# A two-layer gated cross-attention block: six of eight batches' projections moved in among the first half groups of the attention

## The chip, the cores and the metric

The kernel runs on one core of a Trainium2 chip. The metric is the device time of one execution in microseconds. The core has TensorE (PE; its weight loads are shown apart as PEld), VectorE (DVE), ScalarE (ACT), GpSimd (POOL) and SyncE (SP, which here only issues DMAs). Each runs its own instructions strictly in the order in which they are written, and waits where a semaphore has not reached its value.

## The reference

Two gated layers on x (8 batches, 512 tokens, 256 features) with a context of the same shape:

```python
x = x + tanh(g_xattn[0]) * pruned_attention(layernorm(x), ctx)      # 16 heads of 16
x = x + tanh(g_ffn[0])   * fp4_swiglu(layernorm(x))                 # weights and inputs on an FP4 grid
x = x + tanh(g_xattn[1]) * linear_attention(ctx, layernorm(x))      # then a layer norm
x = x + tanh(g_ffn[1])   * int8_linear(layernorm(x))
```

Pruned attention is `softmax(q k^T / 4)`; of its 512 columns the 460 with the largest column sums are kept, the other 52 are zeroed, and the result is multiplied with v. In the linear attention `kv = k^T v` depends on the context alone, so each batch has one 256x256 matrix (`m`) and a row (`r`) that the feed-forward part multiplies with.

## The kernel before

The program has four stages. `prepare` loads and transposes the weights. `project` computes, batch by batch, q, k and v of the attention and the matrix `m` of the linear attention, and writes them to scratch memory in HBM. `attend` and `feed` share one block, `attend_and_feed`: the attention, and behind it the feed-forward units, whose first ones overlap the attention's tail.

**The projection (`project`, L427 to L778).** It is its own block with its own pools: it uses all eight PSUM banks (`psT` two for transposes, `psP` four for products, `psE` two for the matrix part). For one batch TensorE transposes normalized x (L508), computes x1 of the previous batch (L526, L529), transposes the context (L508), multiplies q (L514), kv of the previous batch (L538), k (L514), m of the previous batch (L548 to L553), v (L578) and the gram matrix of the context (L584). ScalarE evacuates xT, cT, the high (fp16) part of q and k, and the gram matrix; VectorE writes the low part (`parts`, L629), v (L690), the statistics and the normalized x (`norm`, L604 to L623), and the small matrix operations. `Fp4Weights` rounds the feed-forward weights to the FP4 grid among this: `scales` on VectorE behind batch 0, `round` (four VectorE operations for a third of the weights) in batches 1, 6 and 7, `split` (two operations) on GpSimd, and at the very end `transposes` on TensorE with `copies` on ScalarE and VectorE.

**The attention (`attend`).** The unit is a half group z, of which there are 256: two 128x512 score tiles in `ps_a`. For each z TensorE makes the first scores (L920), VectorE their negated row maxima (L991), ScalarE two exponentials with row sums (L1090). Every second z, TensorE adds column sums into `ps_c` (L947) with weights from VectorE's reciprocal (L1002). After 16 half groups (one unit) VectorE ranks the column sums in steps of one operation per z (L1034 to L1050) to find the 52 dropped ones. The second scores (L920 into `ps_b`, with shift and drop rows added), their exponential (L1098) and the product with v (L962) of half group z run `LAG = 42` half groups later. So in the first 42 steps, the head, there are first scores only, `ps_b` and `ps_v` are idle, and so is most of TensorE. All engines run the same loop:

```python
            for z in range(at.last):
                step(z)
                n = z - tail
```

SyncE's part (`at.sync`) loads q and k of unit u (`load`, L862), v (`load_values`, L867), and places the shift and drop rows (L877, L885). The first four buffers of q and k are set to 1.0 first: two memsets on VectorE (L984, L985), six on GpSimd.

## Time and profile before

| | |
|---|---|
| median of 3 runs | 1329.58 us (1328.76 to 1330.57) |
| profiled execution, its own time | 1333.29 us |
| its span, first to last instruction | 1331.6 us, mean granted clock 0.927 |
| TensorE busy in the span | 1063.7 us (80%) |
| VectorE busy | 1046.6 us (79%) |
| ScalarE busy | 871.1 us (65%) |
| GpSimd busy | 119.5 us (9%) |

The stages by the trace: `prepare` to 20.4 us, `project` with the FP4 transposes from 20.4 to 229.4, the first score of the attention at 240.9, the first second score at 320.7, the last exponential of first scores at 805.3, the feed-forward part to the end. "Busy" is the time in which an engine has an instruction; a busy TensorE is not TensorE at its peak, and its speed depends on the granted clock, which is 1.0 (2.4 GHz) or 0.5 (1.2 GHz).

### The profile page before, as it was taken

How to read it: one execution, taken by the hardware profiler on the slowest of the kernel's cores; microseconds unless marked ns; L12 is line 12 of the kernel's file. 1: busy time of each engine (PE TensorE's matmuls, PEld its weight loads, DVE VectorE, ACT ScalarE, POOL GpSimd, SP SyncE). 2: the span in 40 equal slices, each digit the busy share in tenths (PEclk: the TensorE clock that was granted, in tenths of full speed). 3: DMA queues.
4: the chain of work that ended last, by engine and by line, in shares of the span. 5: the costliest groups of instructions: out<-in, count | busy, mean ns of one | idle time of the engine just before them, and what ended most of it. 6: DMA issues, size and time to landing. Idle time of an engine off the chain costs nothing.

```text
span 1331.6 us, 17557 instructions
## 1 busy us (share of the span) xinstructions
PE 1063.7 (80%) x5688; PEld 511.6 (38%) x5688; DVE 1046.6 (79%) x2095; ACT 871.1 (65%) x1896; POOL 119.5 (9%) x111
## 2 busy tenths in 40 slices
PE   4999996577677777677777775788999999999985
PEld 3667774011111111111111111234667676676663
DVE  3675664588888988888888885546799999999975
ACT  2232322577999999999999994575454555555542
POOL 0030226200000000000000000000111111110111
PEclk7999997555999999999999998788999999999987
DMA  7444331211121112222221101011011111111000
GB/s 231 137 146 159 136 124 43 48 33 33 30 41 28 32 38 41 42 41 42 41 41 35 36 18 49 15 37 40 25 48 40 33 52 44 32 37 36 25 16 32
DMA packets 77887, 71.77 MB, mean 54 GB/s; under 512 B 13738, under 2 KB 71396, under 8 KB 77796
## 3 DMA queue, kind: packets, MB, share of 16 engines
q1 hardware_dynamic: 77796, 70.65, 19.9%
q8 instruction: 46, 0.75, 0.2%
q14 instruction: 45, 0.37, 0.1%
HBM read 42.83 MB, written 27.28 MB: 53 GB/s over the span
## 4 chain that ended last, share of the span: by engine, by line
ACT 34%; PE 33%; issue 7%; DVE 6%; SPq 1%; DMA 1%; POOL 0%; ACTq 0%; DVEq 0%
ACT ea L1090 20%; ACT prob L1098 13%; PE ps_a L1306 11%; PE ps_b L1265 6%; PE ps_c L1265 4%; PE ps_v L1265 2%; PE ps_a L1286 2%; PE ps_c L947 2%; DVE nmax L991 2%; PE ps_a L1315 1%; PE ps_b L920 1%; PE ps_v L962 1%; PE ps_a L920 1%; PE ps_b L1361 1%; PE ps_c L1258 1%
## 5 line engine op out<-in xcount | busy, mean ns | idle before, releaser
L1090 ACT ACTIVATE ea<-ps_a,nmax 128x512 f32<-128x512 f32 x512 | 362.6, 748 | 31.9 <-DVE nmax L991 31.8
L991 DVE TENSOR_REDUCE nmax<-ps_a 128x2 f32<-128x1024 f32 x256 | 312.9, 1223 | 70.5 <-PE ps_a L920 68.9
L1098 ACT ACTIVATE prob<-ps_b 128x1024 f32<-128x1024 f32 x256 | 279.2, 1091 | 48.7 <-PE ps_b L920 48.7
L920 PE MATMUL ps_b<-q_st,k_st 52*128 52x512 f16 x512 | 102.5, 396 | 143.6 <-ACT prob L1098 143.5
L1306 PE MATMUL ps_a<-wgu,xT 128*128 128x352 f32 x512 | 164.9, 467 | 2.5 <-ACT xT L1430 2.3
L920 PEld LDWEIGHTS ps_b<-q_st,k_st 52*128 52x128 f16 x512 | 25.1, 93 | 368.9 <-ACT prob L1098 336.6
L947 PE MATMUL ps_c<-ea,rz 128*32 128x512 f32 x1024 | 153.7, 676 | 1.1 <-DVE rank L1034 1.1
L962 PE MATMUL ps_v<-prob,v_in 128*16 128x512 f32 x1024 | 137.0, 607 | 11.6 <-DVE att L1058 11.4
L1090 ACT ACTIVATION_READ_ACCUMULATOR ea<-ps_a,nmax 128x1 f32 x512 | 136.2, 266 | 0.0
L920 PE MATMUL ps_a<-k_st,q_st 48*128 48x512 f16 x512 | 108.1, 419 | 31.3 <-ACT ea L1090 18.4
L1306 PEld LDWEIGHTS ps_a<-wgu,xT 128*128 128x128 f32 x512 | 94.7, 192 | 50.4 <-issue 5.1
L1443 ACT ACTIVATE ea<-ps_a 128x352 f32<-128x352 f32 x128 | 59.4, 464 | 76.3 <-PE ps_a L1306 76.2
L1265 PE MATMUL ps_b<-wdn,hT 128*128 128x256 f32 (+1 forms) x384 | 97.1, 392 | 0.0
L1251 POOL TENSOR_TENSOR rs_a<-ve_a,half 128x4 f32<-128x4 f32 x20 | 20.2, 1012 | 755.3 <-DVE ve_a L1576 755.3
L1039 DVE MAX8 top<-rank 128x8 f32<-128x512 f32 x112 | 76.6, 684 | 0.2
L1045 DVE MATCH_REPLACE8 rank<-top,rank 128x512 f32<-128x512 f32 x112 | 75.7, 676 | 0.0
L1265 PEld LDWEIGHTS ps_b<-wdn,hT 128*128 128x128 f32 (+1 forms) x384 | 66.6, 189 | 21.9 <-issue 15.9
L1254 POOL TENSOR_TENSOR rs_b<-ve_b,half 128x4 f32<-128x4 f32 x19 | 37.6, 1978 | 263.6 <-DVE ve_b L1592 263.6
L920 PEld LDWEIGHTS ps_a<-k_st,q_st 48*128 48x128 f16 x512 | 26.0, 96 | 75.5 <-ACT ea L1090 55.6
L1614 DVE SCALAR_TENSOR_TENSOR ea<-ea 128x512 f32<-128x512 f32 (+1 forms) x32 | 36.9, 1155 | 10.7 <-ACT ea L1425 5.8
L962 PEld LDWEIGHTS ps_v<-prob,v_in 128*16 128x16 f32 x1024 | 17.6, 94 | 65.7 <-issue 61.7
L947 PEld LDWEIGHTS ps_c<-ea,rz 128*32 128x32 f32 x1024 | 21.0, 112 | 55.7 <-issue 55.7
(233 smaller groups left out, 1622.8 us busy)
## 6 DMA issues: line engine op xcount, KB each, us to landing
q_scr<-q_p SPq DMA_DIRECT2D x24, 256.0 KB, 2.7
k_scr<-k_p SPq DMA_DIRECT2D x24, 256.0 KB, 2.5
q_st<-q_scr SPq DMA_DIRECT2D x32, 192.0 KB, 4.7
k_st<-k_scr SPq DMA_DIRECT2D x32, 192.0 KB, 5.0
x_in<-in_x SPq DMA_DIRECT2D x8, 512.0 KB, 5.6
c_in<-in_ctx SPq DMA_DIRECT2D x8, 512.0 KB, 4.2
v_scr<-v_s SPq DMA_DIRECT2D x8, 512.0 KB, 2.6
v_in<-v_scr SPq DMA_DIRECT2D x16, 256.0 KB, 3.1
```

Source lines behind the costliest of these rows:

```text
L920: return e.matmul(bank, left[b][o:o + rows, r, t * P:t * P + P], right[b][o:o + rows, r], start=True, stop=True)
L947: e.matmul(ps_c[32 * j:32 * j + 32, :], rz[:, n % TT, n // TT, j], ea[g % RING][:, j], start=(n == 0), stop=(n == GROUPS - 1)).then_inc(s_ ...
L962: e.matmul(ps_v[32 * j:32 * j + DK, :], v_in[u % 2][:, t, o:o + DK], prob[g % RING][:, j], start=(t == 0), stop=(t == TT - 1)).then_inc(s_ ...
L991: e.tensor_reduce(nmax[u % 2][:, t].rearrange("p (h r) -> p r h", h=2)[:, r], ps_a[:, z % 2 * 2:z % 2 * 2 + 2], AX_X, ALU.max, negate=True ...
L1039: e.max(top[:, :], rank[:, :]).then_inc(*dv.up())
L1045: e.match_replace(rank[:, :], top[:, :], rank[:, :], NEG).then_inc(*dv.up())
L1090: e.activation(ea[c % RING][:, g % 4], ps_a[:, g % 4], ACT.Exp, bias=nmax[u % 2][:, t, n:n + 1], accum_out=tot[u % 2][:, t, n:n + 1]).then ...
L1098: e.activation(prob[g % RING][:, 2 * (z % 2):2 * (z % 2) + 2], ps_b[:, :, :], ACT.Exp).then_inc(s_prob, 1)
L1254: e.tensor_tensor(rs_b[p][:, :, :], ve_b[p][:, :, :], half[:, :, :], ALU.pow).then_inc(s_rs_b, 1)
L1265: ins = e.matmul(dst[:, t * D:t * D + D], left(c, t), right(c), start=False, stop=(last and t == N - 1 and c == chunks[-1]))
L1306: ins = e.matmul(gu[:, q % 2, 0:HALF_F], xT[:, c, t * P:t * P + P], w.wgu[:, c, k * HALF_F:(k + 1) * HALF_F], start=(c == 0), stop=(c == D ...
L1443: e.activation(dst[:, t, k % 2 * HALF_F:(k % 2 + 1) * HALF_F], gu[:, q % 2, 0:HALF_F], func).then_inc(s_act_gu, 1)
```

## The change

Everything from the projection on becomes one block. `project` is rewritten as a list of fills. A fill is one piece of work of one PSUM bank: TensorE writes it, ScalarE or VectorE or both take it out, and the next fill of that bank waits for that (`left`). A batch has 16 fills: 0 and 1 xT, 3 and 4 cT, 6 and 7 q, 9 and 10 k, 12 gram, 14 and 15 v, and, for the previous batch, 2 x1, 5 rb, 8 kv, 11 m, 13 row. Fill n uses bank n % 3 of `ps_b[0]`, `ps_b[1]` and `ps_v`, which the attention does not use before step 42. The 32 fills of batches 0 and 1 run first, with all FP4 work beside them, then the FP4 transposes; the other 110 (batches 2 to 7 and the matrix part of batch 7) are spread over steps 0 to 40 of the attention's loop, two or three behind each step.

Other edits: x is normalized in place by ScalarE (`normal`, four 128x256 operations with scale and bias, in two halves) instead of by VectorE, which now also computes the bias `nb`; most double buffers of the projection become single; FP4 rounding works in place; all the feed's and the attention's memory is allocated beside the projection's, except `prob`, which takes its place; the memsets of `q_st` and `k_st` come ahead of the projection on VectorE and GpSimd; GpSimd runs all three splits before the first row of `row_parts`; SyncE's queue interleaves the projection's loads and stores with the attention's first loads; the memset of `ps_v` goes, and the first second scores and the first product with v wait for the last fills of the banks.

```diff
 def build(nc, a, out):
...
-            prepare(nc, ctx, a, w, ey)
-            project(nc, ctx, a, w, ey, scr)
-        attend_and_feed(nc, ctx, a, out, w, scr)
+            prepare(nc, ctx, a, w, ey, [at.ps_a[:, n] for n in range(4)])
+            fp4.with_scales(Mem(nc, early, ctx), [at.ps_a[:, n] for n in range(4)])
+            pj = project(Mem(nc, early, ctx), a, w, ey, scr, [at.ps_b[:, 0], at.ps_b[:, 1], at.ps_v[:, :]])
+        at.prob = [m.sb(f"prob{n}", [P, 4, T]) for n in range(at.ring.shape[1])]
+        fd = feed(m, a, out, w, scr, at)
+        run(nc, ctx, fp4, pj, at, fd)
...
+    FILLS, BANKS = 16, 3
+    ALL = FILLS * B + 14
+    MATRIX = (2, 5, 8, 11, 13)
...
+    def left(n):
+
+        b, k = n // FILLS, n % FILLS
+        if k in MATRIX:
+            return {2: s_dve_x1, 5: s_dve_rb, 8: s_dve_kv, 11: s_act_m, 13: s_dve_row}[k], b
+        if k == 12:
+            return s_act_gram, b + 1
+        s, first = [(s_act_xT, 0), (s_act_cT, 3), (s_dve_q, 6), (s_dve_k, 9), (None, 12), (s_dve_v, 14)][
+            (0, 0, 0, 1, 1, 1, 2, 2, 2, 3, 3, 3, 4, 4, 5, 5)[k]]
+        return s, 2 * b + k - first + 1
...
+    def tensor(e):
...
+        def fill(n):
+            if not real(n):
+                return
+            b, k, dst = n // FILLS, n % FILLS, bank[n % BANKS]
+            p, g = b % 2, n - BANKS
+            while g >= 0 and not real(g):
+                g -= BANKS
+            if g >= 0:
+                e.wait_ge(*left(g))
+            if k < 2:
+                e.wait_ge(s_act_xn, b + 1)
+                transposes(dst, ey.x_in[p], k).then_inc(s_pe_xT, 1)
...
+    def vector(e):
...
+            elif k == 3:
+                if b + 1 < B:
+                    stats(b + 1)
...
+            elif k in (6, 7):
+                if k == 6 and b + 1 < B:
+                    refine(b + 1)
+                e.wait_ge(s_act_q, 2 * b + k - 5)
+                low_part(src, q_p[p], cols[:, 0], k - 6).then_inc(s_dve_q, 1)
...
+    def scalar(e):
...
+            if b + 1 < B:
+                if k == 5:
                     guess(b + 1)
...
+                elif k in (8, 13):
+                    normal(b + 1, k // 13)
...
+def run(nc, whole, fp4, pj, at, fd):
...
+    AHEAD = 2
+    OPEN = 41
...
+        def fills(z):
+
+            first, count = AHEAD * pj.fills, pj.all - AHEAD * pj.fills
+            return range(first + min(z, OPEN) * count // OPEN, first + min(z + 1, OPEN) * count // OPEN)
...
         @block.sync
...
+            fp4.load(e)
+            for b in range(AHEAD):
+                project(b)
+            load_heads(0)
+            load_heads(1)
+            project(2)
+            load_heads(2)
+            project(3)
+            load_values(0)
+            project(4)
+            place_shifts(0)
+            project(5)
+            project(6)
+            place_shifts(1)
+            place_dropped(0)
+            project(7)
+            store_m(7)
...
         @block.gpsimd
         def _(e):
+            row_parts = pj.gpsimd(e)
+            fp4.clear(e)
             at.gpsimd(e)
+            for k in range(3):
+                fp4.split(e, k)
+            for b in range(B):
+                row_parts(b)
...
         @block.tensor
...
+            for n in range(AHEAD * pj.fills):
+                fill(n)
+            fp4.transposes(e)
+            fp4.done(e)
...
             for z in range(at.last):
                 step(z)
+                for n in fills(z):
+                    fill(n)
...
         @block.vector
...
+            stats(0)
+            refine(0)
+            for n in range(AHEAD * pj.fills):
+                fill(n)
+                if n == 7:
+                    fp4.scales(e)
+                if n == 12:
+                    fp4.round(e, 0)
+                if n == pj.fills + 3:
+                    fp4.round(e, 1)
+                if n == pj.fills + 9:
+                    fp4.round(e, 2)
+            fp4.copies(e, 1)
```

How the order on TensorE changes in the head. Before, in the middle of the attention's first 42 half groups, there are only first scores (`ps_a`) and column sums (`ps_c`):

```order
L920 MATMUL ps_a<-k_st,q_st 128x512 x4
L947 MATMUL ps_c<-ea,rz 32x512 x4
L920 MATMUL ps_a<-k_st,q_st 128x512 x4
L947 MATMUL ps_c<-ea,rz 32x512 x4
L920 MATMUL ps_a<-k_st,q_st 128x512 x4
L947 MATMUL ps_c<-ea,rz 32x512 x4
```

Now, on the same engine, steps 8 to 10, with the fills of batch 3 (5 to 7; 8 and 9; 10 and 11) between them:

```order
L951 MATMUL ps_a<-k_st,q_st 128x512 x2
L591 MATMUL ps_v<-wt,c1w 128x256 x2
L563 MATMUL ps_b<-xT,wt 128x512 x4
L951 MATMUL ps_a<-k_st,q_st 128x512 x2
L981 MATMUL ps_c<-ea,rz 32x512 x4
L600 MATMUL ps_v<-x,wt 128x128 x4
L563 MATMUL ps_b<-cT,wt 128x512 x2
L951 MATMUL ps_a<-k_st,q_st 128x512 x2
L563 MATMUL ps_b<-cT,wt 128x512 x2
L611 MATMUL ps_v<-kvs,wq 128x128
L614 MATMUL ps_v<-ident 128x128
```

Each pair of first scores now has a batch's sixth behind it, and the next pair stands behind the products.

On VectorE before, the head holds maxima and reciprocals alone, one pair of maxima after the other:

```order
L991 TENSOR_REDUCE nmax<-ps_a 128x2 x2
L1002 RECIPROCAL rz<-tot 128x4
L991 TENSOR_REDUCE nmax<-ps_a 128x2 x2
L1002 RECIPROCAL rz<-tot 128x4
L991 TENSOR_REDUCE nmax<-ps_a 128x2 x2
```

Now, on VectorE, steps 0 to 2, with fills 2, 3 and 5 of batch 2:

```order
L1025 TENSOR_REDUCE nmax<-ps_a 128x2 x2
L681 SCALAR_TENSOR_TENSOR x<-rows,c,ps_b 128x256 x2
L644 BN_STATS st<-x_in 128x6 x4
L647 BN_AGGR mv<-st 128x2 x4
L649 TENSOR_SCALAR ve<-mv 128x4
L1025 TENSOR_REDUCE nmax<-ps_a 128x2
L689 SCALAR_TENSOR_TENSOR rb<-rows,ps_b 128x256
```

The maximum of a step stands behind the projection work of the step before it, and that work waits for TensorE and ScalarE.

On GpSimd, behind the memsets, the three splits now stand ahead of the first row of the matrix part:

```order
L370 TENSOR_TENSOR dn<-dn,fm 128x1408
L372 TENSOR_TENSOR dn<-dn,fs 128x1408
L547 CAST r_p<-r_s 1x256
L549 TENSOR_TENSOR r_s<-r_s,r_p 1x256
L547 CAST r_p<-r_s 1x256
```

Before, the first split stood ahead of the rows of batches 0 to 6, and the other two behind them.

## Rows read from the trace of the kernel before

**Rows 1.** The page: busy tenths in 40 slices of 33.3 us each.

```profile
PE   4999996577677777677777775788999999999985
...
PEclk7999997555999999999999998788999999999987
```

**Rows 2.** Windows by stage: length, PE, PEld, DVE, ACT, POOL busy us (instructions), clock, DMA.

```profile
20.40:69.60 49.20, 41.02 (x164) 28.75 (x165) 29.18 (x75) 12.76 (x26) 0.56 (x2) 0.86 0.47 154
69.60:219.20 149.60, 134.15 (x637) 100.68 (x636) 94.20 (x216) 41.02 (x87) 45.01 (x42) 0.99 0.39 132
92.60:137.20 44.60, 42.69 (x207) 32.12 (x206) 24.08 (x69) 13.42 (x29) 5.12 (x10) 1.00 0.53 182
...
240.90:320.70 79.80, 60.20 (x238) 8.29 (x239) 66.83 (x108) 59.59 (x169) 0.80 (x7) 0.50 0.13 21
```

**Rows 3.** Groups by line in the head, 240.9 to 320.7 us: busy, mean ns, idle before.

```profile
L991 DVE TENSOR_REDUCE nmax<-ps_a 128x2 f32<-128x1024 f32 x42 | 50.8, 1218 | 19.1 <-PE ps_a L920 18.6
```

**Rows 4.** Timeline, one half group late in the head: start, us, engine, line.

```profile
316.94 1.20 DVE L991 TENSOR_REDUCE nmax<-ps_a 128x2 f32<-128x1024 f32 x1
...
317.89 0.60 PE L920 MATMUL ps_a<-k_st,q_st 48*128 48x512 f16 x2 [1.18 <-ACT ea L1090]
...
318.12 0.68 DVE L1045 MATCH_REPLACE8 rank<-top,rank 128x512 f32<-128x512 f32 x1
318.17 0.69 ACT L1090 ACTIVATE ea<-ps_a,nmax 128x512 f32<-128x512 f32 x1 [0.34 <-DVE nmax L991]
```

**Rows 5.** Timeline of PE, 320 to 322 us: the first second scores.

```profile
320.73 0.61 PE L920 MATMUL ps_b<-q_st,k_st 52*128 52x512 f16 x2
```

**Rows 6.** Timeline of PE in the projection of batch 3.

```profile
97.83 3.60 PE L514 MATMUL psP<-xT,wt 128*128 128x512 f32 x8
...
107.38 3.62 PE L578 MATMUL psP<-wt,cT 128*128 128x256 f32 x16
110.84 3.62 PE L584 MATMUL psP<-c_in 128*128 128x256 f32 x16
114.29 0.93 PE L508 MATMUL psT<-ident,xn 128*128 128x128 f32 x7
```

**Rows 7.** Timeline of DVE in the same batch.

```profile
97.23 0.87 DVE L637 SCALAR_TENSOR_TENSOR x<-rows,c,psE 128x256 f32<-128x256 f32 x2 [3.28 <-PE psE L529]
...
102.77 1.41 DVE L629 SCALAR_TENSOR_TENSOR q_p<-psP,cols,q_p 128x512 f16<-128x512 f32 x2 [4.34 <-ACT q_p L745]
...
104.73 0.42 DVE L651 TENSOR_TENSOR kvs<-kvt,blk 128x256 f32<-128x256 f32 x1
```

**Rows 8.** Timeline of ACT in the same batch.

```profile
93.32 0.83 ACT L726 ACTIVATE m_s<-psE,m_mean 128x256 f32<-128x256 f32 x2
...
101.47 1.27 ACT L745 ACTIVATE q_p<-psP,cols 128x512 f16<-128x512 f32 x2 [2.17 <-PE psP L514]
```

**Rows 9.** Windows over one piece of DVE work each: FP4 scales, one rounding, layer-norm statistics.

```profile
48.30:55.40 7.10, 6.92 (x28) 4.54 (x28) 7.03 (x6) 2.04 (x5) 0.00 (x0) 1.00 0.68 222
71.50:77.10 5.60, 5.35 (x25) 4.06 (x26) 5.50 (x6) 2.29 (x6) 0.00 (x0) 1.00 0.18 66
108.40:110.50 2.10, 2.10 (x12) 1.84 (x11) 1.97 (x10) 0.03 (x1) 0.00 (x0) 1.00 0.52 170
```

**Rows 10.** Timeline, 70 to 84 us: a DVE product beside GpSimd's split.

```profile
77.17 3.44 POOL L368 TENSOR_TENSOR fg<-fq,fm 128x1536 f32<-128x1536 f32 x1 [56.17 <-DVE fq L355]
...
80.69 2.81 POOL L370 TENSOR_TENSOR gq<-fg,fs 128x1536 f32<-128x1536 f32 x1
...
82.19 1.58 DVE L651 TENSOR_TENSOR kvs<-kvt,blk 128x256 f32<-128x256 f32 x1
```

**Rows 11.** Timeline, 229 to 242 us: launch of the attention.

```profile
229.85 1.76 DVE L984 MEMSET q_st<- 128x2048 f16 x1 [1.70 <-PEq L429]
...
233.78 0.66 SPq L862 DMA_DIRECT2D q_st<-q_scr  x1
...
240.94 0.13 PEld L920 LDWEIGHTS ps_a<-k_st,q_st 48*128 48x128 f16 x4 [13.18 <-DMA k_st<-k_scr]
```

696 lines of the change are left out of this document (341 added, 355 removed).

## The prediction

> **What bounds the kernel now.** I read the page's slices first, then a table of windows by stage, then the rows of single instructions in each stage. The slices show three regimes [rows 1]: for 220 us TensorE is at 9 tenths or more with its clock at full speed; then comes a stretch of three slices where it is granted 5 tenths, the 1.2 GHz level; then the steady attention. The windows name them [rows 2]. The projections of batches 2 to 7 take 149.6 us with TensorE busy for 134.2; two of them, free of FP4 work, take 44.6 us with 42.7 busy, so one batch is 22.3 us and 21.3 of TensorE's work. They are TensorE's. The head of the attention (its first 42 half groups, in which the second scores have not begun) takes 79.8 us, 1.90 per half group, with TensorE at 1.2 GHz, VectorE busy for 66.8 and ScalarE for 59.6. There the loop between VectorE's maxima (1.22 us each, 42 of them [rows 3]) and ScalarE's exponentials decides: the exponential waits for the maximum [rows 4], and the maximum for TensorE for 18.6 us in all [rows 3]. The head ends with the first second scores at 320.7 [rows 5]. One stage is one engine's, the other leaves that engine half idle: the change lays one over the other.
>
> **The unit of the sum.** Nothing behind 320.7 us is edited, so the change is worth the shift of this point. It has two parts: when the first score starts (now 240.9 [rows 11]) and how long the head lasts.
>
> **Part 1: the front, up to the first score.** Two batches now end at 69.6, 49.2 us after their block began [rows 2]. Added to them on VectorE: two memsets of 1.8 each, formerly behind the projections [rows 11] and now ahead of the first statistics (3.5), and the three FP4 roundings, of which none stood in this stretch, 5.5 each (16.5) [rows 9]. Their cover was six batches of TensorE's work. It is gone: with three banks TensorE is at most three fills ahead, about 5 us by the products of [rows 6], while the scales (7.0) and a rounding (5.5) [rows 9] are longer than that or as long. Against this stands VectorE's idle time of 20 us in the old stretch (49.2 less 29.2 busy [rows 2]), of which I let 5 be filled, since most of it was waiting for products that are still late. GpSimd adds a stall: beside its split (3.44 and 2.81 us) VectorE's product `kvs` took 1.58 us and ended 0.3 after the split, against 0.42 alone [rows 10, 7]. In the change the second split starts as its rounding ends, and the next VectorE work is the root of the norms, small products of this same kind: up to 6.2 us, which I take in full. Sum: 69.6 + 3.5 + 16.5 + 6.2 - 5 = 90.8 for the end of batch 1. The third split (some 6) begins after the last rounding, late in batch 1, and ends at about 90; only behind it does GpSimd split batch 0's row (2.6 us, an estimate: five small operations of some 0.5 each, near the 0.42 of VectorE's small product [rows 7]), and SyncE's queue has that row's store ahead of the head loads. So the loads are issued at about 93, and the first score follows 7.2 us after the first of them (240.9 less 233.8 [rows 11]): 100. The FP4 transposes, ten us (from 219.2, where the projections end [rows 2], to 229.85, where the attention's memsets begin [rows 11]), lie beside them. Bounds: 92, with no stall on GpSimd, and 108, with none of VectorE's idle time used and 3 us of further stalls. The start moves from 240.9 to 100, by 141.
>
> The Trainium skill (SBUF — State Buffer, section SBUF: two separate sides) has a rule against this change: GpSimd and a VectorE instruction with two SBUF inputs, or in a two-port mode, lock one pair of ports, and the loser blocks for the whole instruction. Rows 10 agree for one instruction. By that rule the first split too would be serial to VectorE's second rounding, another 6 us: the start would be 106, and the time 6 us above my forecast.
>
> **Part 2: the head.** Six steps (half groups) carry exactly one batch of 16 fills, in groups of 2, 3, 3, 2, 3 and 3. What each engine then has per batch, at full clock:
> - TensorE: 21.3 of projection [rows 2], and six steps of the head's own work, 60.2 us at 1.2 GHz over 42 steps [rows 2], so 0.72 at 2.4 GHz and 4.3 for six: 25.6.
> - VectorE: six maxima 7.3 [rows 3]; from the 20th step on six rank operations of 0.68 [rows 4], 4.1; of the batch itself 24.1 us for two [rows 2], or 12.0. Normalizing x (on ScalarE now) leaves, and split reductions and the root's fifth operation come, about even: 19.3 early, 23.4 late.
> - ScalarE: exponentials 59.6/42 = 1.4 per step [rows 2], 8.5; 6.7 for its projection work [rows 2], and four normalizing operations, at the 0.83 of two 128x256 ones [rows 8], 1.7: 16.9.
>
> So TensorE is the floor, 25.6 per batch. But engines run in the written order, and each waits for the others through three banks. I follow the chain through one late batch. (1) VectorE in the second step: maxima 1.2, rank 0.7, x1 0.9 [rows 7], statistics 2.0 [rows 9], then the next maxima 1.2: 6.0. (2) ScalarE: two exponentials 1.4, the root's guess 0.4, both evacuations of q 1.27 [rows 8]: 3.1. (3) VectorE: low part of q 1.4 [rows 7], half of it beside ScalarE, c1w 0.5 and a part of the root: 1.7. (4) Fourth step: maxima 1.2, exponentials 1.4, normalizing 0.8, evacuation and low part of k 0.65 and 0.7: 4.8. (5) Only that low part frees the bank of the gram product: 3.45 on TensorE (107.38 to 110.84 is such a piece [rows 6]), next step's score and column sums 1.3, the row product 0.4, 0.8 of waiting for the bank that ScalarE leaves, and the values 3.45: 9.4. (6) Last values on VectorE 0.7, maxima 1.2, rank 0.7: 2.6. Sum 27.6; eight hand-overs between engines, at 0.03 to 0.2 each (the maximum ends at 318.14, its exponential starts at 318.17; the score ends at 318.49 [rows 4]), say 1.0: 28.6 per late batch. In an early one two rank operations are missing from the chain: 27.2. Three of each: 167. The last six steps carry only the matrix part of batch 7: VectorE has 1.9 per step, 11.5, and 5 of matrix work: 16.5. The head thus starts at 100, and lasts 167 + 16.5 = 183.5, and 4.5 more for a clock that will be at 1.2 GHz when it starts, after the wait for the loads, and must rise: 188. It ends at 288, against 320.7.
>
> **Edits that I cost at nothing.** The stores and loads of batches 2 to 7 stand in SyncE's queue in the order in which their data comes, each load a batch (28 us) ahead of its use; without this cover a load of 512 KB would show. The `place_shifts` waits are passed before the batch behind them is due. The rank work was there before. The clock at the joint with the steady attention is no worse: TensorE comes from work, not from the half clock.
>
> **Sum.** 288 - 320.7 = -32.7 against the profiled span of 1331.6. Its execution took 1333.3 us, the median of the runs is 1329.6, 3.7 lower; I take the shift from the median: 1297.
>
> **Rivals.**
> (A) **TensorE's floor**: the three banks are enough, the chain is hidden, and GpSimd stalls nobody. Start 92, head 6 x 25.6 + 16.5 = 170: 262, a gain of 58.5: 1271. For it: the projections reach 96% of TensorE before [rows 2]. Against it: they had eight banks and only VectorE's and ScalarE's own work behind them.
> (B) **Lockstep**, slower than before: if VectorE waits for ScalarE's evacuation in every step, and ScalarE for VectorE's next maximum, their work adds up: 23.4 + 16.9 = 40.3 per batch late and 36.2 early, head 230 + 16.5 + 4.5 = 251. It ends at 351, 30 later: 1360. The place is the pair of high and low part, fills 6, 7, 9 and 10. It decides from where a batch costs (320.7 - 100 - 21)/6 = 33.3 us. For it: before, in the head, the two engines already alternate [rows 3, 4]. Against: only two or three of six steps hold such a pair, and in the others VectorE owes ScalarE nothing.
> (C) **Half lockstep**: 31.5 per batch and a start at 106: ends at 316, a gain of 5 to 20: 1310 to 1325.
> (D) **The clock does not rise** in the head since TensorE idles between fills: at 1.2 GHz a batch costs 51 us of TensorE, 306 for six, and the time is 1430. Before, TensorE had 2.4 GHz at 0.7 of its time busy [rows 1]; at 25.6 of 28 it should have it here.
> That the change doesn't do what it says I rule out: the order of the instructions shows it.
>
> **How the numbers follow.** Forecast 1297, with its own bounds 1284 to 1310 (start 92 to 108, a batch 27 to 29.5): 0.58. A, 1271 to 1284: 0.14. C: 0.16. B and what lies between: 0.10, with D 0.02. The range that holds 8 in 10 reaches into A and C: 1276 to 1322. A measurement of this kernel can tell some 0.2% (2.7 us) from no change. Faster by more than that: 0.58 + 0.14 + 0.14 = 0.86; within it 0.03; slower 0.11.
>
> **What would show it.** In the new profile: first score at 92 to 108 us; the first `ps_b<-q_st,k_st` scores at 275 to 300; the clock at 10 tenths in the head; 27 to 29.5 us between two batches' gram products; TensorE busy over 85% there; VectorE's rounding and GpSimd's splits apart from each other, and `rs`, `tmp` products behind the second split late by up to 6 us. The steady attention stays at 484.8 us and the feed at its length. I am wrong if a batch takes over 31 us, if the head's clock shows 5 tenths beyond its first 10 us, or if the time behind the second scores changes by more than 3 us.

## The result, and the profile after

| | before | after |
|---|---|---|
| median of the runs, side by side | 1330.07 us (4 runs) | 1297.18 us (1296.81 to 1297.85, 4 runs) |
| ratio, 95% interval | | 0.9754 (0.9737 to 0.9771) |
| span of the profiled execution | 1331.6 us | 1296.1 us |
| first transposes of x | 25.5 us | 31.3 us |
| first score | 240.9 us | 105.8 us (forecast 100) |
| length of the head | 79.8 us | 180.6 us (forecast 188) |
| first second scores | 320.7 us | 286.4 us (forecast 288) |

The forecast was 1297, and the change gives 1297.2: 32.9 us less than before. Two terms of the sum were off by 6 and 7 us, and cancelled: each lies within its own bounds, but that the total agrees to 0.2 us is luck.

The page's slices of the changed kernel, 32.4 us each:

```profile
PE   2868999987777776776776775888999999999985
...
PEclk8878999998999999999999997788999999999987
```

Against [rows 1], the stretch at 5 tenths of the clock is gone: the head, from 105.8 to 286.4 us, has TensorE at 8 and 9 tenths and the clock at 9 (which is 90% or more) once its first slice is over. What is left of low clock stands in the first four slices and around the joint with the feed.

Windows by stage of the changed kernel: length; PE, PEld, DVE, ACT and POOL busy us (instructions); granted clock; DMA share; GB/s. The first two are the front (batch 0, then batch 1 with the FP4 work), the next two one early and one late batch of the head, then the steady attention from the first second scores on, and the rest:

```profile
31.30:58.30 27.00, 20.94 (x64) 13.88 (x65) 17.93 (x21) 8.17 (x17) 4.06 (x2) 0.78 0.31 98
58.30:96.60 38.30, 25.92 (x101) 17.77 (x100) 28.62 (x41) 8.90 (x19) 17.53 (x11) 0.82 0.28 90
...
153.09:180.54 27.45, 27.34 (x137) 16.66 (x137) 18.11 (x43) 16.61 (x44) 2.49 (x5) 1.00 0.45 135
208.00:235.60 27.60, 27.17 (x137) 16.41 (x138) 21.96 (x52) 16.71 (x43) 2.48 (x5) 1.00 0.44 151
...
286.40:772.40 486.00, 345.35 (x2554) 57.47 (x2558) 431.41 (x764) 484.10 (x1085) 3.30 (x11) 0.99 0.21 42
772.40:1296.10 523.70, 465.60 (x2028) 301.55 (x2020) 413.90 (x910) 263.53 (x515) 59.10 (x39) 0.94 0.12 35
```

The front shows the gap: batch 0 has TensorE busy for 20.9 of 27.0 us and batch 1 for 25.9 of 38.3, at 0.78 and 0.82 of the clock. In the head TensorE is busy for 27.3 of 27.45 us per batch. Taken alone that row says that TensorE bounds the head; the experiments show why it must not be read so. VectorE's low part of k, a row that starts at 152.29 and takes 0.75, ends at 153.04, and the gram product that needs its bank starts at 153.09. The steady attention keeps its length: from the first exponential of second scores (290.4; before 323.6) to the last one of first scores (772.2; before 805.3) it is 481.7 us, as before.

The timeline of TensorE in the changed kernel at the points on which the forecast was laid: first transposes, first score, two batches' gram products (L619), first second scores. In brackets the idle time before a row and what ended it:

```profile
31.32 1.97 PE L558 MATMUL ps_b<-ident,x_in 128*128 128x128 f32 x8 [12.59 <-ACT x_in L755]
...
105.76 0.61 PE L951 MATMUL ps_a<-k_st,q_st 48*128 48x512 f16 x2 [4.09 <-DMA k_st<-k_scr]
...
125.65 3.72 PE L619 MATMUL ps_v<-c_in 128*128 128x256 f32 x16 [0.44 <-DVE k_p L668]
...
153.09 1.13 PE L619 MATMUL ps_b<-c_in 128*128 128x256 f32 x4
...
286.38 0.39 PE L951 MATMUL ps_b<-q_st,k_st 52*128 52x512 f16 x2
```

The gram products start at 125.65, 153.09, 180.54, 207.99, 235.59 and 263.10, so a batch takes 27.45 us early and 27.5 to 27.6 late. The groups by line in the head:

```profile
L1124 ACT ACTIVATE ea<-ps_a,nmax 128x512 f32<-128x512 f32 x82 | 55.7, 687 | 69.0 <-DVE nmax L1025 69.0
L1025 DVE TENSOR_REDUCE nmax<-ps_a 128x2 f32<-128x1024 f32 x42 | 51.0, 1217 | 8.7 <-PE ps_a L951 8.6
```

[Rows 3] had the maxima wait 19.1 us, nearly all for TensorE's scores; now they wait 8.7 us, and the exponentials of ScalarE wait 69.0 us for the maxima. The loop between these two engines, which was the old head, no longer sets the pace; VectorE has the fills' work ahead of its maxima.

### The profile page after: what moved, and what is told of

Same layout as the page of the kernel before. It is cut to its first block, busy times and chain, and to the rows that moved or that the text cites. A ratio compares the mean times of both kernels' runs of the same rounds, so it can differ in the third digit from the quotient of the medians.

```text
span 1296.1 us, 17705 instructions
## 1 busy us (share of the span) xinstructions
PE 1045.4 (81%) x5688; PEld 507.7 (39%) x5688; DVE 1041.7 (80%) x2086; ACT 884.1 (68%) x1935; POOL 111.7 (9%) x111
## 3 DMA queue, kind: packets, MB, share of 16 engines
q1 hardware_dynamic: 77796, 70.65, 20.9%
## 4 chain that ended last, share of the span: by engine, by line
PE 42%; ACT 36%; DVE 11%; issue 8%; SPq 1%; DMA 1%; POOL 0%; ACTq 0%; DVEq 0%
ACT ea L1124 20%; ACT prob L1132 14%; PE ps_a L1339 11%; PE ps_b L1298 6%; PE ps_c L1298 4%; PE ps_v L1298 2%; PE ps_a L1319 2%; PE ps_b L629 2%; PE ps_b L619 2%; PE ps_b L563 1%; PE ps_a L1348 1%; DVE nmax L1025 1%; PE ps_c L981 1%; PE ps_v L997 1%; PE ps_b L951 1%
## 5 line engine op out<-in xcount | busy, mean ns | idle before, releaser
L981 PE MATMUL ps_c<-ea,rz 128*32 128x512 f32 x1024 | 138.1, 612 | 0.0
L951 PE MATMUL ps_a<-k_st,q_st 48*128 48x512 f16 x512 | 99.3, 384 | 7.0 <-DMA k_st<-k_scr 4.1
L1079 DVE MATCH_REPLACE8 rank<-top,rank 128x512 f32<-128x512 f32 x112 | 75.7, 676 | 0.0
L1298 PEld LDWEIGHTS ps_b<-wdn,hT 128*128 128x128 f32 (+1 forms) x384 | 66.6, 189 | 21.9 <-issue 15.9
```

What stands on the lines that cost most here:

```text
L951: return e.matmul(bank, left[b][o:o + rows, r, t * P:t * P + P], right[b][o:o + rows, r], start=True, stop=True)
L981: e.matmul(ps_c[32 * j:32 * j + 32, :], rz[:, n % TT, n // TT, j], ea[g % RING][:, j], start=(n == 0), stop=(n == GROUPS - 1)).then_inc(s_ ...
L1079: e.match_replace(rank[:, :], top[:, :], rank[:, :], NEG).then_inc(*dv.up())
L1298: ins = e.matmul(dst[:, t * D:t * D + D], left(c, t), right(c), start=False, stop=(last and t == N - 1 and c == chunks[-1]))
```

## The experiments

Times are medians; ratios are to the kernel before, run on the same chip beside each. The theory on record is the chain through VectorE, ScalarE and TensorE; the row with 27.3 of 27.45 us gave its rival, TensorE's floor. Each kernel has one profile. Four of the edits (q_half, stats_twice, stats_less, both_less) touch nothing ahead of the first score, and yet it came at 106.9, 105.6, 104.6 and 105.3 us; a difference of 1 us in one profile of the front is therefore no evidence.

### q_half: TensorE's q product halved from batch 2 on

```diff
-                into(dst, WQ, xT, k - 6).then_inc(s_pe_q, 1)
+                if b < 2:
+                    into(dst, WQ, xT, k - 6).then_inc(s_pe_q, 1)
+                else:
+                    e.matmul(dst, wt[:, WQ, 0, (k - 6) * P:(k - 6) * P + P], xT[:, 0], start=True,
+                             stop=True).then_inc(s_pe_q, 1)
```

> From batch 2 on, the q product of each fill has one matmul instead of two (half of its contraction is left out); nothing of VectorE's, ScalarE's or the queues' work changes. It takes about 0.9 us off each of 12 fills (two q fills take 3.64 us). Theory 'chain' (the one on record: VectorE, ScalarE, VectorE and TensorE by turns set 27.5 us per batch, and the q product lies beside the chain): 0 to -2 us. Theory 'floor' (TensorE's own instructions are all of the 27.5 us): -1.8 us per batch, -9 to -11 us in all, and 25.7 us from one batch's gram products to the next.

Measured: 1296.15 us (1294.0 to 1299.3), ratio 0.9742 (0.9719 to 0.9764). The window of the same batch, and TensorE's gram and k products in it (columns as above):

```profile
153.06:180.51 27.45, 25.90 (x132) 15.97 (x132) 18.12 (x43) 16.59 (x44) 2.49 (x5) 1.00 0.44 135
```

```profile
153.06 3.72 PE L623 MATMUL ps_b<-c_in 128*128 128x256 f32 x16 [0.44 <-DVE k_p L672]
...
174.51 1.98 PE L563 MATMUL ps_b<-cT,wt 128*128 128x512 f32 x4 [1.11 <-DVE q_p L672]
```

TensorE is busy for 25.9 us instead of 27.3, and the batch takes 27.45 us as before, to the hundredth. The time taken away comes back as two waits: 1.11 us before the k product, for VectorE's low part of q, and 0.44 before the gram product, for its low part of k. Only the last interval, 25.9 us instead of 27.5, got shorter. In four of five intervals TensorE's work did not decide; the last one is taken up below.

### stats_twice: VectorE's statistics issued twice

```diff
-            for t in range(TT):
-                e.bn_stats(st[p][:, t], ey.x_in[p][:, t]).then_inc(*dv.up())
-            e.wait_ge(*dv.now())
+            for _ in range(1 if b < 3 else 2):
+                for t in range(TT):
+                    e.bn_stats(st[p][:, t], ey.x_in[p][:, t]).then_inc(*dv.up())
+                e.wait_ge(*dv.now())
```

> The four bn_stats of batches 3 to 7 are issued twice, so VectorE has 1.6 us more in each of five batches, 8.2 us in all; TensorE has nothing more. Theory 'chain': +7 to +8 us, since the statistics stand in the first link of the chain. Theory 'floor': 0 to +2 us, VectorE being busy for 18 to 22 of 27.5 us per batch.

Measured: 1305.80 us, ratio 0.9814 (0.9797 to 0.9831), 8.6 us above the change. One batch:

```profile
155.39:184.28 28.89, 27.61 (x136) 16.73 (x136) 19.52 (x47) 16.59 (x44) 2.49 (x5) 1.00 0.41 129
```

The extra work is 1.44 us (eight operations took 2.84 us, four 1.40), and the second and third interval between gram products are 1.44 us longer, 28.89 instead of 27.45, although VectorE is busy for only 19.5 us of it. The first and the fourth are 1.1 and 1.3 us longer, and the fifth, without statistics, 0.1. The head is 6.8 us longer, and the time 8.6, a little over the 7 to 8 expected; the profile has the other 2 us at the joint with the feed, of which more below.

### stats_less and both_less: VectorE's work cut, alone and with TensorE's

```diff
-            for t in range(TT):
+            for t in range(TT if b < 3 else 1):
                 e.bn_stats(st[p][:, t], ey.x_in[p][:, t]).then_inc(*dv.up())
```

Three of a batch's four token groups are then normalized with stale statistics. both_less has this and the edit of q_half.

> For batches 3 to 7 only one of four bn_stats is issued (the norms of x then use stale statistics of three of four token groups); VectorE has 1.1 us less in each of five batches. New theory 'two equal bounds': the chain through VectorE and ScalarE and TensorE's own instructions are each 27.4 us per batch, so shortening one alone gives nothing: 0 to -1 us, gram products still 27.4 apart, TensorE without a wait before them. 'Chain alone': -5 to -6 us.

> Both cuts together: half of the q product's contraction left out from batch 2 on (0.9 us per fill on TensorE), and three of four bn_stats of batches 3 to 7 left out (1.1 us per batch on VectorE). 'Two equal bounds': each alone gives 0 to -1 us, both together -5 to -7 us, 26.4 us per batch, the chain's own length. 'Chain alone': about -6 us too, but then the statistics alone gave as much. 'Neither decides': 0 to -2 us.

Measured: stats_less 1294.04 us, ratio 0.9732 (0.9718 to 0.9747); both_less 1291.29 us, ratio 0.9707 (0.9693 to 0.9722). One early batch of stats_less, and one of both_less:

```profile
150.90:177.75 26.85, 26.85 (x138) 16.51 (x137) 17.35 (x40) 16.70 (x44) 2.48 (x5) 1.00 0.44 138
```

```profile
149.54:176.00 26.46, 25.89 (x132) 15.97 (x132) 17.12 (x40) 16.59 (x44) 2.49 (x5) 1.00 0.45 140
```

Here the two bounds come apart. With 1.0 us less on VectorE (one operation took 0.42 us, four 1.40) the batch takes 26.85 us, and TensorE is busy for all 26.85: that is its floor. With TensorE's work cut as well it is 26.46, that is 27.45 less 0.99, the chain's own length. So the chain sets the 27.45, and TensorE's floor lies 0.6 us below it. My new theory of two equal bounds was wrong by that 0.6: the statistics alone gave 3.1 us where I had said 0 to 1 (2.3 of them in the head; the first score came 1.2 earlier, with which the edit has nothing to do). From 208.0 us on, with the rank operations, it is different: in the fourth interval either cut alone leaves 27.5 and both together 26.5, so there the bounds stand within 0.1; in the fifth, which has no statistics, the cut on TensorE alone gives 25.9. The late bound of 27.5 is not TensorE's work alone, which is the same as early. In stats_less TensorE waits there before its q product, for ScalarE's read-out of cT:

```profile
220.87 3.70 PE L563 MATMUL ps_b<-xT,wt 128*128 128x512 f32 x8 [0.43 <-ACT cT L776]
```

What makes up the rest of the 0.65 us by which 27.5 exceeds 26.85 was not tried.

### two_banks: the third bank taken away

```diff
-    FILLS, BANKS = 16, 3
+    FILLS, BANKS = 16, 2
```

VectorE also clears the third bank once at the start.

> The fills go round two PSUM banks instead of three (the third is only cleared once), everything else as in the change. Theory 'the third bank carries the merge': each fill then waits until the fill two before it is read out, which takes a turn of ScalarE and VectorE behind the maxima and exponentials; 29 to 34 us per batch, +10 to +40 us in all, and an idle time of TensorE before its fills that ends with ScalarE's or VectorE's copies. Rival 'one fill of slack is enough': a fill with the scores between is 1.5 to 2.5 us, as long as a copy, and the time rises by less than 5 us.

Measured: 1346.21 us, ratio 1.0117 (1.01 to 1.0134): 1.2% slower than before, and 49 us above the change, where 10 to 40 had been expected. TensorE's gram product and x1 in one batch:

```profile
141.54 5.41 PE L619 MATMUL ps_b<-c_in 128*128 128x256 f32 x16 [2.37 <-DVE k_p L669]
...
156.25 1.99 PE L582 MATMUL ps_b<-wt,gram 128*128 128x256 f32 x8 [1.13 <-ACT xT L771]
```

A batch takes 34.2 us early and 32.4 to 34.1 late, since TensorE now waits before single fills: in this batch 2.37 us before the gram product, 1.13 before x1, 0.5 to 0.7 before others. Clock was lost too: it is 0.95 over the batch, and the gram product behind its wait takes 5.41 us instead of 3.72. 40 us are the head's and 10 the front's. The prediction had worked out that the merge loses its gain at 33.3 us per batch; with two banks the batch is at that price, and the gain is gone. The third bank is what the merge lives on.

### not_merged: all fills ahead of the attention

```diff
-            return range(first + min(z, OPEN) * count // OPEN, first + min(z + 1, OPEN) * count // OPEN)
+            return range(0)
...
-            for n in range(AHEAD * pj.fills):
+            for n in range(pj.all):
...
             for b in range(AHEAD):
                 project(b)
+                if 4 <= b < 7:
+                    load_heads(b - 4)
```

AHEAD is 8, the second diff line stands for TensorE, VectorE and ScalarE alike, and SyncE's list is reordered accordingly.

> All fills, in the same three banks and order, run before the attention's first half group; the head loads are issued before the last batch is stored. This keeps the rebuilt projections and takes the merge away. Theory 'all of the gain is the merge, the rebuild costs or gives little': the fills go at TensorE's 22 us per batch, the first score comes at about 235 (96.6 + 6 x 22.3 + 5), the head lasts 80 us at 1.2 GHz as before, second scores at 315 to 320: 1323 to 1330 us. Rival 'the rebuild itself gives part of it': first score before 225, below 1318. Rival 'three banks are too few even alone, and the attention's steps only hide it': over 24 us per batch, above 1335.

Measured: 1331.75 us, ratio 1.001 (0.9996 to 1.0023), no change against before, and 2 us above the range that I had expected. One batch, and the head:

```profile
154.63:175.96 21.33, 21.24 (x102) 15.79 (x101) 11.39 (x34) 8.90 (x19) 2.49 (x5) 1.00 0.75 198
242.15:321.70 79.55, 59.54 (x238) 8.35 (x240) 66.83 (x108) 59.70 (x169) 0.22 (x5) 0.53 0.01 1
```

The batch takes 21.33 us, before it was 22.3 [rows 2]: three banks in rotation are enough for the projections alone. The microsecond per batch went, as far as the profile shows, into a later start (first transposes at 32.3 instead of 25.5) and an uncovered end (the last batch's matrix part stands alone, with four waits from 0.5 to 1.3 us, and the transposes of the FP4 weights follow), so the first score comes at 242.2 instead of 240.9. The head is 79.5 us at half the clock, as [rows 2]. So the rebuild by itself is worth nothing, and the merge is worth 35 us: second scores at 321.7 here, at 286.4 in the change. The Trainium skill (Perfetto Trace Analysis, Matmul Optimizations) asks for all eight PSUM banks to be used. By that rule three would have cost something here; these rows show no cost for the projections alone.

### early_heads: the head loads ahead of two stores in SyncE's queue

```diff
             if b + 2 < B:
                 load_c(b + 2)
+            if between is not None:
+                between()
             if b:
                 store_m(b - 1)
             store_v(b)
...
             for b in range(AHEAD):
-                project(b)
-            load_heads(0)
-            load_heads(1)
+                project(b, heads if b == 1 else None)
```

> SyncE issues the eight loads of the first two head groups (both of batch 0) ahead of batch 0's row store and batch 1's value store; all engines' work is unchanged. Theory 'the loads wait in SyncE's queue behind GpSimd's row split' : issued at about 85 instead of 98, landed by 95, so that the first score comes when TensorE has done the FP4 transposes, at 101.7 to 102.5 instead of 105.8: -3 to -4 us. Rival 'the start is bounded by the transposes' copies or by VectorE': 0 to -1 us.

Measured: 1291.69 us, ratio 0.971 (0.9693 to 0.9727), 5.5 us below the change, more than the 3 to 4 expected. SyncE's queue and TensorE's first score:

```profile
88.92 0.69 SPq L895 DMA_DIRECT2D q_st<-q_scr  x1
...
94.86 0.29 SPq L522 DMA_DIRECT2D r_scr<-r_p  x1
...
102.97 0.39 PE L953 MATMUL ps_a<-k_st,q_st 48*128 48x512 f16 x2 [0.96 <-ACT wdn L420]
```

The loads go out at 88.9 instead of 98.0, and the first score follows the transposes at once, 2.8 us earlier. The rest is the clock. In the change TensorE had waited 4.1 us for the loads, and its next 19.89 us, up to the first gram product, ran at 0.85 of the clock. Here the same work took 17.15 us at 1.00. The windows of the change and of early_heads:

```profile
105.76:125.65 19.89, 19.06 (x75) 11.50 (x75) 12.11 (x31) 11.02 (x29) 0.00 (x0) 0.85 0.40 92
```

```profile
102.97:120.12 17.15, 16.62 (x74) 9.55 (x74) 12.11 (x31) 10.85 (x29) 0.00 (x0) 1.00 0.26 80
```

So behind the wait the clock cost 2.7 us more. The edit moved the loads ahead of both stores at once and does not say which store held them up by how much.

### late_split: the second rounding moved away from the small operations

```diff
-                if n == pj.fills + 3:
+                if n == pj.fills + 7:
                     fp4.round(e, 1)
```

> As early_heads, and VectorE's second FP4 rounding moves from behind fill 19 to behind fill 23, so that the root of batch 2's norms (five small operations) runs ahead of it and not beside GpSimd's second split. Theory 'shared port': the two products of 3.3 and 2.7 us are 0.16 us again, the k product of batch 1 no longer waits 5.8 us, and batch 1 ends some 5 us earlier; the last split and with it the transposes end 2 to 3 us earlier: first score at 98 to 100, -6 to -8 us against the change. Rival 'the stall only moves': the operations then beside the split (low parts of k, sums and means) are held up instead, and the time is within 1.5 us of early_heads.

Measured: 1291.23 us, ratio 0.9706 (0.969 to 0.9722), 0.5 us below early_heads, within their scatter. VectorE's two stalled instructions behind the rounding, and the TensorE product that waits for the first:

```profile
74.90 3.23 DVE L714 TENSOR_TENSOR kvs<-kvt,blk 128x256 f32<-128x256 f32 x1
...
78.71 3.56 DVE L354 TENSOR_TENSOR dn<-dn,fs 128x1408 f32<-128x1408 f32 x1
...
78.28 0.77 PE L613 MATMUL ps_b<-kvs,wq 128*128 128x128 f32 x2 [6.94 <-DVE kvs L714]
```

The root's operations took 0.16 us each again, but `kvs` (0.42 alone) now takes 3.23 beside GpSimd's split, and the third rounding's first product 3.56 instead of 1.61; TensorE waits 6.94 us for `kvs`. The rival was right that the stall moves, though mostly not to the operations that it named. Of the 6.94 us only 2.8 are the stall of `kvs`; most of the rest is the rounding itself, 68.8 to 74.3, which now stands ahead of `kvs`. My "6 to 8 us" was an argument from the two operations held up and not from what VectorE does next.

### pool_memsets: VectorE's two memsets given to GpSimd

```diff
-        for n in range(1, BUFS):
+        for n in range(BUFS):
...
-        e.memset(q_st[0][:, :, :], 1.0).then_inc(s_set[0], 1)
-        e.memset(k_st[0][:, :, :], 1.0).then_inc(s_set[0], 1)
```

> As early_heads, and the two memsets of q_st and k_st (1.76 us each) that stand ahead of VectorE's first statistics move to the end of GpSimd's other memsets. Theory 'they are on the path of the start': VectorE's first statistics begin at 20.6 instead of 24.7, the first transposes come at 27 instead of 31, and all behind them 4 us earlier: 1287 to 1288 us. Rival 'GpSimd's memsets hold VectorE up anyway' (its small operations of 0.17 us took 0.5, 0.9 and 1.4 us beside them): 1 to 2 us of it come back, 1289 to 1290. Rival 'the FP4 loads or scales set the pace of the front': no change.

Measured: 1289.72 us, ratio 0.9689 (0.9672 to 0.9707), 2.0 us below early_heads. TensorE's first transposes:

```profile
26.91 1.97 PE L560 MATMUL ps_b<-ident,x_in 128*128 128x128 f32 x8 [9.09 <-ACT x_in L757]
```

They come at 26.9 instead of 30.7 in early_heads, and the second scores at 276.3 instead of 280.9, so the front did gain its 4 us and more, although VectorE's small operations were again held up beside GpSimd's memsets (1.22, 0.86 and 1.36 us instead of 0.17), as the first rival had said. In the profiles the joint, 480 us later, is 2.7 us longer. The time falls into the range of the first rival (1289 to 1290), but not for its reason. (The edit puts the two memsets ahead of GpSimd's other `q_st` and `k_st` memsets, not behind them.)

### ahead3: three batches ahead of the attention

```diff
-    AHEAD = 2
+    AHEAD = 3
...
-                if n == pj.fills + 3:
+                if n == 23:
                     fp4.round(e, 1)
-                if n == pj.fills + 9:
+                if n == 39:
                     fp4.round(e, 2)
```

GpSimd splits batch 0's row ahead of its third FP4 split, and SyncE's list follows.

> As pool_memsets, with three batches ahead of the attention instead of two, the FP4 roundings behind fills 12, 23 and 39, and GpSimd's row split of batch 0 ahead of its third FP4 split. TensorE has some 12 us of waiting in batch 1 beside the FP4 work; three batches should hide most of it. Front +21.3 us (a batch alone, as in not_merged) less 8 to 12; head: of the 27.45 us per batch 11.4 belong to six half groups at 1.9 (79.5 us for 42 in not_merged), so a batch less is worth 16 by the chain and 20.4 by TensorE. Sum by the chain -3 to +5 us against pool_memsets, by TensorE's floor -8 to +1.

Measured: 1297.06 us, ratio 0.975 (0.9735 to 0.9764), 7.3 us above pool_memsets: outside both expected ranges. The whole head:

```profile
120.35:283.60 163.25, 153.67 (x774) 90.72 (x775) 120.91 (x268) 97.57 (x257) 12.45 (x25) 0.98 0.26 85
```

The start moves by 21.9 us, from 98.4 to 120.4, instead of by 21.3 less 8 to 12, so nothing at all was hidden: the two later roundings are followed by waits of 6.94 and 6.34 us for `kvs`, as in late_split. The head is 14.7 us shorter (163.2 instead of 177.9). 16 was expected of the chain and 20.4 of TensorE; TensorE is busy for 153.7 of the 163.25 us. Which of the two decides here was not tested.

### scales_later and scales_split_later: where the FP4 work stands in the front

```diff
-                if n == 7:
+                if n == 10:
                     fp4.scales(e)
-                if n == 12:
+                if n == 15:
                     fp4.round(e, 0)
```

Both stand on pool_memsets; scales_split_later has late_split's edit too.

> As pool_memsets; VectorE's FP4 scales (7 us) move from behind fill 7 to behind fill 10 of batch 0, and the first rounding from behind fill 12 to behind fill 15, so that the low parts of k go first and TensorE has the gram product and the values (7.2 us) beside the scales. Theory 'the place, not the amount, of the FP4 work costs the front': the wait of 6.04 us of TensorE before the gram product goes, 1 to 3 us come back before the transposes of batch 1: first score 3 to 5 us earlier, at 94 to 96, 1285 to 1287 us (the clock at the joint with the feed adds or takes up to 3 us). Rival 'VectorE is the front's bound': the wait moves behind the rounding, at most 1 us is gained.

> As scales_later, with the second rounding behind fill 23 instead of 19, as in late_split. There the stall beside the second split only moved and 1 to 2 us were gained; with the first rounding later, the second one behind fill 19 would start beside the first split and be held up itself (as the third was in late_split: its first product took 3.56 us instead of 1.61). Expected: 1 to 3 us below scales_later; rival: no difference, since TensorE then waits for the masked product behind the rounding (6.9 us in late_split).

Measured: scales_later 1289.54 us (1285.4 to 1290.7), ratio 0.9687 (0.9663 to 0.9712), no change against pool_memsets, as the rival had it; scales_split_later 1284.94 us (1284.37 to 1285.43), ratio 0.9658 (0.9644 to 0.9673), 4.6 us below scales_later where 1 to 3 were expected. TensorE's waits of the latter, from batch 0's values to the first score:

```profile
48.07 0.65 PE L560 MATMUL ps_v<-ident,x_in 128*128 128x128 f32 x4 [1.72 <-DVE v_s L740]
...
54.89 2.07 PE L593 MATMUL ps_b<-wt,c1w 128*128 128x256 f32 x4 [3.37 <-DVE x L683]
...
72.38 0.77 PE L613 MATMUL ps_b<-kvs,wq 128*128 128x128 f32 x2 [6.70 <-DVE kvs L714]
...
84.07 6.13 PE L631 MATMUL ps_b<-wt,cT 128*128 128x256 f32 x16 [2.75 <-ACT m_s L793]
...
96.07 0.39 PE L953 MATMUL ps_a<-k_st,q_st 48*128 48x512 f16 x2 [0.96 <-ACT wdn L420]
```

The 6.04 us before batch 0's gram product are gone in both. In scales_later they came back: the first split now ran beside the statistics and the second rounding's start, and waits of 3.4, 4.9 and 5.1 us stood in batch 1. There GpSimd was held up too: its second operation took 4.27 us instead of 2.81 beside a rounding product of VectorE that had started 0.15 us ahead of it. With the second rounding moved as well, the root runs ahead of it, and the waits of 4.9 and 5.1 give way to one of 6.70 us for `kvs`; the first score comes at 96.1 instead of 99.0. scales_split_later beats both kernels of this case: 12.2 us below the change, 45 below before.

## Why the prediction was right, point by point

**What bounds each stage.** Right. The steady attention did not move, and the time moved by the shift of the second scores: 34.3 us in the profile. The medians give 32.9; the execution profiled of before was 3 us above its median, as the prediction had noted. One word ahead of it needs care: most of TensorE idle, said of the old head, holds for the work at full clock only; at half the clock TensorE was busy for 60.2 of 79.8 us [rows 2].

**Part 1, the front: 100, measured 105.8.** The terms were these.
- Memsets, 3.5: the first transposes came 5.8 us later. 4.3 are the memsets with the gaps around them (VectorE's `ones` are set from 20.23 to 20.40, and its statistics begin at 24.7). The rest are VectorE's small operations, held up beside GpSimd's memsets (0.50 and 0.87 us instead of 0.17), and ScalarE's normalizing of 2.08 us in place of VectorE's 1.38.
- The stall beside the second split, up to 6.2: met. The mechanism is in these rows of the changed kernel: POOL's two split operations, VectorE's root, TensorE's k product and values; then SyncE's row store, value store and first head load.

```profile
69.61 3.42 POOL L370 TENSOR_TENSOR gn<-gn,fm 128x1536 f32<-128x1536 f32 x1 [8.10 <-DVE gn L360]
69.78 3.27 DVE L656 TENSOR_TENSOR tmp<-rs 128x4 f32<-128x4 f32 x1
...
73.09 0.16 DVE L658 TENSOR_TENSOR tmp<-tmp,ve 128x4 f32<-128x4 f32 x1
73.12 2.81 POOL L372 TENSOR_TENSOR gn<-gn,fs 128x1536 f32<-128x1536 f32 x1
73.29 2.66 DVE L660 TENSOR_SCALAR tmp<-tmp 128x4 f32<-128x4 f32 x1
...
77.06 3.78 PE L563 MATMUL ps_b<-cT,wt 128*128 128x512 f32 x4 [5.75 <-DVE q_p L668]
...
88.69 1.96 DVE L723 TENSOR_SCALAR m_mean<-m_sums 128x2 f32<-128x2 f32 x1
...
91.58 5.19 PE L629 MATMUL ps_b<-wt,cT 128*128 128x256 f32 x16 [2.75 <-ACT m_s L791]
...
96.03 0.25 SPq L522 DMA_DIRECT2D r_scr<-r_p  x1
97.52 0.33 SPq L516 DMA_DIRECT2D v_scr<-v_s  x1
97.97 0.67 SPq L893 DMA_DIRECT2D q_st<-q_scr  x1
```

  `tmp` takes 3.27 us from 69.78 and ends with the split's first half; the third takes 2.66 and ends with the second. Beyond 0.16 each that is 5.6 us, and `m_mean` adds 1.8 beside the third split, which I had not counted. TensorE waits 5.75 and 2.75 us for them.
- The end of batch 1, 90.8: measured 96.6, 5.8 later. Three things in the rows would make up 5.7 of it: 2.3 is the start above, 1.8 is `m_mean`, and 1.6 the value product, which ran at a mean clock of 0.70 after its wait and took 5.2 us instead of 3.6 [rows 6]. This split is a reading and was not tested: other products were slow too (the k product after its wait ran at 0.50, 3.6 us to the next one instead of 1.8), and how much of the roundings' 16.5 us was hidden, for which I had let 5 be filled, no run shows. What is plain is that the term had clock losses of the old stretch only (0.86 [rows 2]), and the new one, with TensorE busy for 47 of 65 us, ran at 0.78 and 0.82.
- The loads: issued at 98.0 and not 93, behind the row store (96.0) and, which I had not named, batch 1's value store (97.5), and the first score 7.8 us behind them and not 7.2. This is the path to the first score: the third split ended at 93.3 and not 90, the row took 2.8 us and not 2.6, and the value store put 1.9 us between row store and loads. early_heads shows that the two stores together held the loads up.

From the Trainium skill's rule (SBUF — State Buffer, section SBUF: two separate sides) I had worked out a start of 106. The start came there, but not by that step: the first split ran from 55.2 to 61.5, and the second rounding began at 64.0, so these two never met. In scales_later, where they did meet, both were held up. The rule itself fits the rows here: beside the splits, held up were VectorE's products with two SBUF inputs, and `tensor_scalar` from SBUF to SBUF, which I take to run in a two-port mode; products with one input in PSUM and `bn_stats` kept their time, and so did `tensor_scalar` of a single element (`r_mean`, 0.14 us). Beside GpSimd's memsets only `tensor_scalar` was held up, and `tensor_tensor` was not. For this case the prediction had the rule too wide: the same section of the Trainium skill counts two SBUF inputs only against a GpSimd instruction that reads SBUF, and a memset reads none.

**Part 2, the head: 188, measured 180.6.** The chain decides, as the prediction said: a microsecond more on VectorE's statistics, link 1, is a microsecond more per batch, and a microsecond less on TensorE's q product, which lies beside the chain, is nothing (in four of five intervals). Only link 1 was tried in this way; ScalarE's links were not. The chain's lengths were 27.2 early and 28.6 late; measured 27.45 and 27.5 to 27.6. The late one was too long: the rank operations, for which I had added 1.4 us, cost 0.1 to 0.2, since they fill VectorE's waits. Six batches are 165 instead of 167. The rest of the head took 15.6 where I had 21: the clock cost 2.7 and not 4.5, by early_heads, and the last steps 12.9 and not 16.5. The 4.5 had no row of this case behind it; in the change the clock stood at half for the first 6 us of the head.

**TensorE's floor** was mis-sized as well: 25.6 in the prediction, 26.85 by stats_less. The projections' share was right (21.33 in not_merged). The step that failed is the division of 60.2 us by two for the full clock: at 2.4 GHz two scores take 0.32 us of TensorE and the column sums 1.0 every second step (starts at 156.75, 157.07 and 158.06 in the changed kernel), which is 4.9 for six steps where I had 4.3. The 0.6 that remain were not traced to any row. The mechanism of rival A was thus nearer than its chance of 0.14 says: 0.6 us per batch, less than 4 us in all, lay between chain and floor. Its time of 1271 was not, for it rested on a floor of 25.6. The floor does not enter the sum; the agreement of the total rests on errors of +5.8 and -7.4 us in the two terms that do.

**The other rivals.** B needs a wait in nearly every step; two_banks, with waits before many fills, has 34.2 us per batch and 1346 us, and still not B's 36 to 40 and 1360. Of C the start came (105.8 against its 106), its 31.5 per batch did not. D did not come either: the clock was at full speed 6 us into the head. The head's batches show nothing of the edits costed at nothing; the value store ahead of the loads did cost in the front, and it stands in no term of the prediction.

**Behind the second scores** I had called over 3 us a refutation: it is 1.2 us shorter. The joint, below, is 2.0 shorter and what follows it 0.4; against that, the first exponential of second scores comes 4.1 us behind the first second score, and came 2.8 behind it before.

## What to carry over

Before you lay one stage over another, sum up the chain through all engines and each engine's own floor, and test them by taking a microsecond from one, then from the other: a busy share of 99% did not mean that TensorE decided. Where work is taken out from under its cover, put it back piece by piece where the waiting engine has products of its own to do, and look at what VectorE does next beside GpSimd's work: moving one piece alone only moved the wait. Order a queue by who is waited for, and add to a wait of TensorE what its clock loses behind it (2.7 us behind one of 4.1 here).

## What was not expected of the hardware

**The joint of attention and feed has a length of its own.** From the last exponential of first scores to the last one of second scores the same instructions run in every kernel. Windows over it, of before, the change, q_half and pool_memsets:

```profile
805.30:912.40 107.10, 78.24 (x371) 28.10 (x367) 48.06 (x112) 58.34 (x75) 4.13 (x4) 0.82 0.11 30
```

```profile
772.20:877.30 105.10, 76.17 (x371) 26.45 (x367) 48.04 (x112) 58.35 (x76) 4.12 (x4) 0.82 0.11 31
```

```profile
769.60:873.40 103.80, 75.65 (x371) 26.29 (x367) 48.11 (x112) 58.32 (x75) 4.12 (x4) 0.84 0.11 31
```

```profile
762.00:869.30 107.30, 78.64 (x371) 28.13 (x367) 48.18 (x112) 58.37 (x76) 4.12 (x4) 0.81 0.11 30
```

It takes from 103.8 to 107.3 us, with TensorE busy for 75.7 to 78.6 and the clock at 0.81 to 0.84; what lies behind it is 418.8 to 419.2 us in thirteen of the fourteen profiles (420.0 in one). In steps of 10 us the granted clock falls and rises several times here (0.59, 0.55, 1.00, 0.63, 0.69 in the change; 0.72, 0.60, 0.83, 0.75, 0.57 before). My reading is that the same work gets another share of full clock as it starts at another time; that is not shown. Each kernel has one profile, and runs of one kernel differ as much (q_half 1294.0 to 1299.3), so the length may change from one execution to the next as well. Either way, up to 3.5 us of the difference between two profiles of this family come from there: 2.0 of the change's gain, and 2.7 us between early_heads and pool_memsets. What sets the pattern was not tried.

**TensorE's busy time hid its waits.** In the change it is busy for 27.34 of 27.45 us, with no wait shown before the gram product; by stats_less the same work takes 26.85. The missing half microsecond is in gaps of 0.1 to 0.3 us between rows that the trace counts as busy (the four m products before the gram product take 1.60 us in the change and 1.34 in stats_less). The Trainium skill says (Perfetto Trace Analysis, opening note) that the matmul row is a bad metric for how close a kernel is to roofline, because matmuls are pipelined. The pair of runs shows something akin, with a number: the row hid waits of half a microsecond in 27.
